# Post-norm attention and feed-forward layer, one core: scaling of probabilities, V's bound and rounded q and k moved to other places of the schedule

## The reference

```
q, k, v = x @ Wq + bq, x @ Wk + bk, x @ Wv + bv     # 16 heads of width 128
q = rotary(q * 128**-0.5); k = rotary(k)            # t*cos + rotate_half(t)*sin
p = softmax(causal(q @ k.T))
x = layernorm(x + (p @ v) @ Wo + bo)
h = silu((x @ w_gate) * s_gate) * ((x @ w_up) * s_up)   # int8 weights, 1024 wide
x = layernorm(x + (h @ w_down) * s_down)
```

## Time and profile before

| | |
|---|---|
| median of 3 runs | 1923.18 us (1920.52 to 1923.53) |
| profiled execution | 1920.36 us, its span 1918.6 us |
| mean granted TensorE clock | 0.990 of full speed |
| busy share of the span | PE 93%, ACT 83%, DVE 82%, POOL 65% |

### The profile page before, as it was taken

How to read it: one execution, slowest core, us unless ns; L and a number is a source line. 1 busy time by engine, 2 the same in 40 slices (tenths; PEclk the granted TensorE clock), 3 DMA queues, 4 the chain that set the end, 5 groups by cost and what they waited for, 6 DMA issues and landing times. The chain is left out here.

```text
span 1918.6 us, 33748 instructions
## 1 busy us (share of the span) xinstructions
PE 1778.1 (93%) x10464; PEld 1406.3 (73%) x10464; DVE 1573.9 (82%) x3748; ACT 1591.1 (83%) x2910; POOL 1246.2 (65%) x1041
## 2 busy tenths in 40 slices
PE   6899999989999999999999999999999999989997
PEld 5677777767777777767777777777777776768886
DVE  6788888888888888888888888888888888876886
ACT  6888888888899888889988899888898988863443
POOL 4667776677666667776767766677766666624554
PEclk8999999999999999999999999999999999989999
DMA  3655565556555656565555655765656775550001
GB/s 97 157 110 111 110 130 114 112 117 134 113 114 116 137 116 110 111 145 116 117 114 104 133 114 114 138 131 115 115 104 110 158 131 100 98 121 12 23 23 34
DMA packets 638257, 210.01 MB, mean 109 GB/s; under 512 B 609408, under 2 KB 622208, under 8 KB 636672
## 3 DMA queue, kind: packets, MB, share of 16 engines
q1 hardware_dynamic: 614400, 165.91, 45.2%
q10 hardware_dynamic: 23680, 41.95, 7.3%
HBM read 48.40 MB, written 8.39 MB: 30 GB/s over the span
## 5 line engine op out<-in xcount | busy, mean ns | idle before, releaser
L848 DVE SCALAR_TENSOR_TENSOR planes<-S,recip,planes 128x128 f16<-128x128 f32 (+7 forms) x512 | 417.3, 815 | 94.0 <-ACT planes L657 91.2
L657 ACT ACTIVATE planes<-S,recip 128x128 f16<-128x128 f32 (+7 forms) x512 | 379.0, 740 | 129.8 <-DVE recip L899 115.9
L423 POOL TENSOR_TENSOR swap<-swap,sin_t 128x512 f32<-128x512 f32 x256 | 331.3, 1294 | 190.4 <-ACT swap L665 190.2
L648 ACT ACTIVATE S<-p_row,neg_max 128x128 f32<-128x128 f32 (+7 forms) x512 | 380.0, 742 | 51.7 <-DVE neg_max L838 44.5
L838 DVE CUSTOM_DVE_ANT_0 p_row<-S,mask_row 128x128 f32<-128x128 f32 (+7 forms) x512 | 385.1, 752 | 27.8 <-PE S L1112 26.3
L417 POOL TENSOR_TENSOR rot<-rot,swap 128x512 f32<-128x512 f32 x252 | 323.0, 1282 | 72.4 <-DVE rot L889 69.8
L665 ACT ACTIVATE swap<-S,bqk 64x512 f32<-64x512 f32 x512 | 349.8, 683 | 18.7 <-DVE wmax L706 5.9
L1112 PE MATMUL S<-QKA 128*128 128x512 f32 (+4 forms) x1152 | 262.7, 355 | 5.0 <-DVE rot L889 4.5
L1112 PE MATMUL S<-QKB 128*128 128x512 f32 (+4 forms) x1152 | 259.6, 352 | 2.6 <-DVE planes L848 2.2
L439 POOL TENSOR_TENSOR QKA<-rot,QKA 128x512 fp32r<-128x512 f32 x124 | 160.1, 1291 | 122.3 <-ACT QKA L491 122.1
L1063 PE MATMUL O<-PT,VB 128*128 128x512 f16 (+3 forms) x1152 | 217.6, 330 | 22.8 <-issue 14.2
(11 more groups left out here) (129 smaller groups left out, 2931.2 us busy)
## 6 DMA issues: line engine op xcount, KB each, us to landing
w_raw<-in_w_heads ACTq DMA_DIRECT2D x64, 256.0 KB, 2.7
wv_raw<-in_w_heads ACTq DMA_DIRECT2D x32, 256.0 KB, 3.5
PT<-planes SPq DMA_TRANSPOSE x512, 3.4
wo_raw<-in_wo_heads ACTq DMA_DIRECT2D x32, 256.0 KB, 3.8
attn_d<-resid ACTq DMA_DIRECT2D x4, 1024.0 KB, 6.7
x_raw<-in_x_cols SPq DMA_DIRECT2D x3, 1024.0 KB, 5.9
resid<-in_x_rows ACTq DMA_DIRECT2D x3, 1024.0 KB, 5.4
resid<-in_x_rows SPq DMA_DIRECT2D x2, 1024.0 KB, 6.7
```

The source lines that it names most:

```text
L423: nc.gpsimd.tensor_tensor(swap[:, c, :], swap[:, c, :], sin_t[:, half], ALU.mult).then_inc(sin_done, 1)
L648: nc.scalar.activation(row_psum(n, s)[:, 0:cols], p_row[:, k % 2, 0:cols], ACT.Exp, bias=neg_max[:, s:s + 1], scale=-1.0, accum_out=row_su ...
L657: nc.scalar.activation(row_halves(n, s)[:, 0], row_psum(n, s)[:, 0:cols].rearrange("p (j q) -> p j q", q=P), ACT.Copy, scale=recip[:, s:s ...
L848: nc.vector.scalar_tensor_tensor(halves_of[:, 1], row_psum(n, s)[:, 0:cols].rearrange("p (j q) -> p j q", q=P), recip[:, s:s + 1], halves_ ...
```

## The change

In ACT's program `probs_high(n, s)` leaves step s and stands at the start of step s + 1 (for the last row, at the start of the next timeline). In DVE's program the reciprocal of a row's sum comes after the cosine product of the same step. The bound of pairs after the first goes to column 511 of the first bank of the score buffer that row 1 of the even head uses (that row fills 256 columns); PE makes it in step 1 just ahead of that row's matmuls, DVE reads it with the new `take_bound` ahead of masking the row, and `scale_up` follows in step 1; weigh moves to step 5 of the odd head before. Waits that kept bound and output apart in bank X are dropped. For heads from n = 0 on, POOL instead of ACT makes the rounded copy of `rot` into `QKA` or `QKB`, and goes on with the low part.

```
-    bound_psum, fold_psum = X[:, GQ - 1:], X[:, 0:DIM]
+    fold_psum = X[:, 0:DIM]
+    def bound_psum(pair):
+        return X[:, GQ - 1:] if pair == 0 else row_psum(2 * pair - 2, 1)[:, GQ - 1:GQ]
...
 # GpSimd
                     if project and 3 <= s < 7 and n >= 0:
-                        pool.wait_ge(rot_hi, n_four(m, c))
+                        pool.wait_ge(rot_done, n_four(m, c))
+                        nc.gpsimd.tensor_copy(q[:, c % 2, 0, half], rot[:, c, :]).then_inc(rot_hi, 1)
+                        pool.wait_ge(rot_hi, n_four(m, c))
...
 # ScalarE
                 for s in range(8):
+                    if s == 0 and prev:
+                        probs_high(n - 1, 7)
+                    if s > 0 and own:
+                        probs_high(n, s - 1)
...
-                    if own:
-                        probs_high(n, s)
...
-                    if project and 3 <= s < 7:
+                    if project and n < 0 and 3 <= s < 7:
...
 # VectorE
+            def take_bound(pair):
+                dve.wait_ge(bounded, pair + 1)
+                wait(dve, scaled, 3 * pair)
+                nc.vector.tensor_scalar(bound[:, :], bound_psum(pair), 1e-30, 1.0 / UP, ALU.max, ALU.mult
+                                        ).then_inc(scaled, 1)
             def scale_up(pair):
-                dve.wait_ge(bounded, pair + 1)
-                nc.vector.tensor_scalar(bound[:, :], bound_psum, 1e-30, 1.0 / UP, ALU.max, ALU.mult
-                                        ).then_inc(scaled, 1)
                 dve.wait_ge(scaled, 3 * pair + 1)
...
-                dve.wait_ge(scaled, 3 * pair + 2)
...
                         dve.wait_ge(scored, n_scored(n, s))
+                        if makes_v(n) and par == 0 and s == 1:
+                            take_bound((n >> 1) + 1)
...
-                    if own:
-                        reciprocal(n, s)
-                    if own and makes_v(n) and par == 0 and s == 6:
+                    if own and makes_v(n) and par == 0 and s == 1:
                         scale_up((n >> 1) + 1)
                     if project and 1 <= s < 5:
                         rotate_cos(n, m, s - 1)
...
-                    if own and makes_v(n) and par == 0 and s == 3:
-                        weigh((n >> 1) + 1)
+                    if own:
+                        reciprocal(n, s)
+                    if par == 1 and s == 5 and makes_v(n + 1):
+                        weigh((n + 3) >> 1)
...
 # TensorE
                 pe.wait_ge(weighed, pair + 1)
-                if pair == 1:
-                    pe.wait_ge(v_lo, n_v_all(0))
-                elif pair > 1:
-                    pe.wait_ge(added, n_added(2 * pair - 2, 0))
...
-                elif i == 1 and makes_v(nn):
-                    pe.wait_ge(scaled, 3 * (nn >> 1) + 4)
...
+                    if makes_v(n) and par == 0 and s == 1:
+                        bound_of((n >> 1) + 1)
                     cols = (s + 1) * P
...
-                    if own and makes_v(n) and par == 0 and s == 6:
-                        bound_of((n >> 1) + 1)
```

More of the change, by code:

```diff
@@ L712, in weigh @@
                                         ).then_inc(weighed, 1)
+            def take_bound(pair):
[3 more added lines that the diff above has]
+                                        ).then_inc(scaled, 1)
             def scale_up(pair):
                 at = slice(pair % 2, pair % 2 + 1)
-                dve.wait_ge(bounded, pair + 1)
-                nc.vector.tensor_scalar(bound[:, :], bound_psum, 1e-30, 1.0 / UP, ALU.max, ALU.mult
-                                        ).then_inc(scaled, 1)
                 dve.wait_ge(scaled, 3 * pair + 1)
                 nc.vector.reciprocal(v_up[:, at], bound[:, :]).then_inc(scaled, 1)
-                dve.wait_ge(scaled, 3 * pair + 2)
-                nc.vector.tensor_scalar(pv_down[:, pair % 3:pair % 3 + 1], bound[:, :], 1.0 / UP, None, ALU.mult).then_inc(scaled, 1)
+                nc.vector.tensor_scalar(pv_down[:, pair % 3:pair % 3 + 1], bound[:, :], 1.0 / UP, None, ALU.mult
+                                        ).then_inc(scaled, 1)
             dve.wait_ge(bias_in, 16)
@@ L788, in run @@
                     if n < 0 and s == 4:
+                        take_bound(0)
                         scale_up(0)
@@ L1043, in bound_of @@
                 pe.wait_ge(weighed, pair + 1)
-                if pair == 1:
-                    pe.wait_ge(v_lo, n_v_all(0))
-                elif pair > 1:
-                    pe.wait_ge(added, n_added(2 * pair - 2, 0))
                 for t in range(KT):
-                    last = mm(bound_psum, ones[:, :], bprod[:, t:t + 1], start=t == 0, stop=t == KT - 1)
+                    last = mm(bound_psum(pair), ones[:, :], bprod[:, t:t + 1], start=t == 0, stop=t == KT - 1)
                 last.then_inc(bounded, 1)
@@ L1141, in values @@
                     elif n == 1 and i == 0:
-                        pe.wait_ge(scaled, 4)
+                        pe.wait_ge(v_lo, n_v_all(0))
                     elif n > 0:
```

## The result

The kernel after takes 1854.88 us, median of 4 runs (1852.92 to 1857.15), beside 1921.85 for the kernel before (4 runs). The ratio is 0.9655, 95% interval 0.9643 to 0.9667: 67 us faster, where 51 were forecast. The predicted 1871 is 16 us too high; the range of 1848 to 1902 holds the time.

A forecast was written before the change was run, and what follows sets the result against it. PE, busy 93%, was taken as the bound: holes of 3.33 us a pair fall to 1.40, and 1.93 less slower starts leaves 1.63. Over 31 pairs that is 51 us, forecast 1871, range 1848 to 1902.

The forecast's parts named there:

- (b): PE's hole at step 1 of the even head, 0.23 us a pair, forecast to go.
- (c): PE's hole at even head's step 5, waiting for V's low half: 0.92 us, to go with weigh's move.
- (d): PE's hole before the bound's matmuls, waiting for the add into resid: 1.38 us, to go with the bound's move.
- Hole (a): PE's hole at even head's step 0, before the products with V: forecast to grow from 0.80 to 1.40 us.
- the product of weigh: DVE's 128x2 product at its new place: 0.6 us expected, 1.3 together with weigh's reduction.
- The walk through mask, exponential, reciprocal and low half: Weigh's delay followed through the odd head's rows 6 and 7: mask 0.9 us late, output's low half 0.6 late.
- the 0.3 taken off for matmuls that start slower when they didn't wait: Deduction from PE's gain per pair: three times 0.1 us, leaving 1.63 of 1.93.
- the product of 2.14 us: DVE's longest 128x2 product, basis of the rival that weigh stays long at its new place: 1897 us, chance 0.15.
- nothing, hidden by that wait: Price of probs_high one step later: weight roundings fall where ACT waits 0.42 us for the reciprocal anyway.
- Nothing: Price of DVE's reciprocal after the cosine product; uncovered it would cost 0.4 us a head, 25 in all.
- limited PE only through (a) and (b): Claim that taking 5 of ACT's 46.4 us a pair brings nothing beyond those two holes.
- POOL's copies: Eight rounded copies of q and k a pair on POOL, 0.75 us each, hidden behind PE.

The follow-up runs named there:

- e3: Kernel before with only the bound's and weigh's move, copies and order as before: 1922.95 us, ratio 1.0013.
- e1: Kernel after with the rounded copies of q and k made by ACT again: 1888.13 us, ratio 0.9836 to before.
- e9: Kernel before with only the new order (probs_high a step later, reciprocal after the cosine product): 1885.29 us, ratio 0.9810.
- e2: Kernel after with the old order of scaling and reciprocal, so bound, weigh and copies changed: 1879.79 us, ratio 0.9787 to before.
- e4: Kernel before with only the rounded copies of q and k moved to POOL: 1895.97 us, ratio 0.9873.
- e6: Kernel after with weigh's 128x2 product replaced by two 128x1 products with a per-partition scalar: 1845.28 us, ratio 0.9605 to before.
- e10: e3 plus one ACT copy of 128x512 a head in step 5, read by nobody: 1945.20 us, ratio 1.0123 to before.

## Why the prediction was right in sum, and where it was wrong

*Holes of PE.* (b), (c) and (d) are gone as said. Hole (a) was forecast at 1.40 and is 1.34; the product of weigh at 0.6 and is 0.598 at the median; weigh together 1.3, measured 1.22 from start to the next start. The walk through mask, exponential, reciprocal and low half held to 0.1 us. The predicted pair was 49.87, the measured 49.60. The last step of the sum has a slip: 1923.2 less 51 is 1872, not 1871.

*The size of the steady gain,* 1.90 for 1.63. The term mis-sized is the 0.3 taken off for matmuls that start slower when they didn't wait. It is 0.12 for the output (1.62 by 1.50), but V's matmuls take 1.43 now (1039.22 to the next group at 1040.65) where they took 1.54 with their wait, so the term is about nothing. (b) was measured by the profile's idle time, 0.23, and from start to start was 0.38 (1.76 from 1026.25 to 1028.01, where the odd head needs 1.38). Against these the odd head's own hole grew by 0.2. There are 14 such pairs: about 4 us.

*Pairs that aren't steady.* The forecast gave all 31 the same 1.63. The early pairs, in which V's bias is folded into the output's, went from 52.33 to 50.26, 2.07 each; the two pairs around each batch boundary gained 4.9, 6.2 and 5.4 together where 3.3 was forecast (for the second, 54.81 + 52.06 against 50.20 + 50.43). These are about 3 and 7 us more. The last three pairs, which the forecast didn't look at, went from 160.1 together to 149.5, 6 us more than forecast; why wasn't looked into. The first pair gained 1 us less than forecast, and the forecast counted 31 pairs where 30 lie between the bounds, 2 us. So 4, 3, 7 and 6 less 1 and 2 make 17, the miss against 1872. The prediction quoted a cost of a batch boundary, the product of 2.14 us, and used it for a rival but not for the sum; the longest in the kernel after is 1.23. How much of the 7 us is this was not measured apart.

*The step that was wrong* is the price of the new order: ACT's part ("nothing, hidden by that wait"), DVE's part ("Nothing") and, with them, that ACT "limited PE only through (a) and (b)". The order alone is worth 36 us, the copies alone 25, and the bound with weigh, to which the prediction gave nearly all of the gain, nothing by itself (e3) and nothing on top of the order (e1, 1888.13 by e9's 1885.29); on top of the copies it is worth 16 (e2 by e4). The reading behind it was right in its facts: the roundings do fall into ACT's 0.42 us wait. But a wait that is filled is time won for the instructions that used to come after it, if the engine is near its limit, and ACT was: 46.4 us of work, 4.0 of waits for reciprocals and 0.8 for row maxima in a pair of 51.5. In a steady pair closing DVE's holes alone gives 0.2 us (e3), the copies alone 0.7 (e4), the order alone 1.0 (e9), and all together 1.9.

That the forecast of the whole came out so near is in part luck. Its sum holds for the kernel after, where the holes (b), (c) and (d) are closed and (a) is as forecast; as an account of which part brings the gain it fails. The gains of e4 and e9 alone add up to 61 of the 67 us. If they added up in one kernel too, the bound's move would be worth little there; but (c) and (d) were still open in both, 0.54 and 1.26 in e9, so it may be worth more. The kernel with order and copies but the old bound was not run, and what the bound adds on top of both stays open.

*POOL's copies* cost 0.615 instead of 0.75 and are hidden, as said; POOL's busy time rose by 4.7 us a pair (8 x 0.615 is 4.9).

## What to carry to other kernels

Before a sum of PE's holes is called the gain, add up each other engine's round as well, its work and those of its waits that it can't avoid (here the 0.42 us between a result and its scale factor), and do it for each head of a pair; where that comes near the period, as ACT's did here, holes that are closed can open elsewhere, as in e3. A wait in an engine that works in order costs nothing only if nothing useful is queued behind it; putting independent work into such waits was part of an edit worth 25 us as the last one and 36 as the only one. An additional instruction that nobody reads, put into two kernels, tells whether an engine has slack at that place, if the clock is looked at as well. And of three parts of a change each should be taken out once; here one wasn't.

## What the runs showed of the hardware

A VectorE product of two 128x2 SBUF tensors took 0.16 us, or lasted to the end of GpSimd's running instruction (within 0.03 us in 90 of 90 cases), 2.14 at the most; with a per-partition scalar as the second operand the 128x1 product took 0.20 to 0.22 in all of 64 cases of e6. A GpSimd copy of 128x512 from float32 to rounded float32 takes 0.615 us, less than half of its two-input instruction (1.29) and as long as ACT's copy (0.62). TensorE's granted clock fell to 0.50 in e10 after PE had stood for 2.00 us before 1068.26, and stayed at full after it had stood for 1.99 us before 964.71.
